# A graph network on one Trainium2 core: in the attention passes of kind "add", the sum over eight edge slots moves from TensorE and ScalarE to one strided VectorE instruction

## What is computed

```python
# layer 0, expert scorer: h is (M, HEADS=4, NUM_EXPERTS=4)
e = leaky_relu(a_src[src] + a_dst[dst], negative_slope=0.2)
ee = exp(e - segment_max(e, dst)[dst])
alpha = ee / (segment_sum(ee, dst)[dst] + 1e-16)
agg = segment_sum(h[src] * alpha[:, :, None], dst)
...
# layer 3: s is (N, 8), Vh is (N, 8, 32)
alpha = leaky_relu(s[src] + s[dst], NEG_SLOPE)
e = exp(alpha - segment_max(alpha, dst)[dst])
a = e / segment_sum(e, dst)[dst]
attn = segment_sum(Vh[src] * a[:, :, None], dst).reshape(N, D_MODEL)
```

## Time and profile before

| | us |
|---|---|
| unprofiled executions (3), median | 13737.19 |
| lowest, highest | 13736.53, 13757.31 |
| profiled execution, its own time | 13846.6 |
| profiled execution, its span | 13844.9 |
| pass `be` in it (first gather to last `add`) | about 4823 to 5915 |
| pass `ge` in it (first gather to last `add`) | about 11336 to 12861 |

### The profile page before, as it was taken

The page is one execution under the profiler, slowest core; times in us unless marked ns, Lnnn a source line. Parts: engine busy times, 40 slices in busy tenths (PEclk is TensorE's granted clock), DMA queues, the critical chain, the costliest instruction groups (busy, mean ns, idle before and its releaser), DMA issues. The chain is left out here.

```text
span 13844.9 us, 108219 instructions
## 1 busy us (share of the span) xinstructions
PE 7534.6 (54%) x30838; PEld 6003.5 (43%) x30838; DVE 6330.2 (46%) x16971; ACT 1340.8 (10%) x3400; POOL 6032.2 (44%) x6195
## 2 busy tenths in 40 slices
PE   3333433346665455586777564545544936666535
PEld 2333333335554345554566433333433835555423
DVE  6555654558886422232112245656522134454454
ACT  0000000000000100011122010000011200010001
POOL 1666366046664066603666406656301036666000
PEclk9999999777777655587788786777776967777767
DMA  1111111046666011202333602212523323336000
GB/s 41 53 51 54 38 54 44 13 139 172 178 178 134 13 8 8 8 14 68 92 90 90 60 13 48 47 41 44 27 26 97 109 58 93 95 94 86 19 7 16
DMA packets 454853, 872.00 MB, mean 63 GB/s; under 512 B 172059, under 2 KB 267149, under 8 KB 453907
## 3 DMA queue, kind: packets, MB, share of 16 engines
q0 software_dynamic: 277568, 621.62, 21.4%
q1 hardware_dynamic: 176714, 243.62, 6.1%
HBM read 820.84 MB, written 52.88 MB: 63 GB/s over the span
## 5 line engine op out<-in xcount | busy, mean ns | idle before, releaser
L552 POOL DMA_INDIRECT ee_rows<-e_table,net_mr_data x1000 | 993.6, 994 | 1038.7 <-POOLq L1656 469.2
L552 POOL DMA_INDIRECT ge_rows<-g_table,net_mr_data x1000 | 959.0, 959 | 674.2 <-issue 241.7
L855 POOL DMA_INDIRECT ce_rows<-c_table,net_mr_data x1000 | 947.2, 947 | 511.6 <-issue 245.5
L387 POOL DMA_INDIRECT main_slots<-em_load,em_where x784 | 809.6, 1033 | 642.5 <-DVE em_where L362 395.6
L552 POOL DMA_INDIRECT ae_rows<-a_table,net_mr_data x752 | 722.5, 961 | 592.5 <-POOLq L1656 202.4
L589 PE MATMUL ee_part_ps<-ee_message,net_eye 125*125 125x256 f32 x2000 | 607.8, 471 | 523.6 <-issue 300.8
L552 POOL DMA_INDIRECT be_rows<-b_table,b_br_data x728 | 696.2, 956 | 434.7 <-issue 172.9
L589 PE MATMUL ge_part_ps<-ge_rows,net_eye 125*125 125x256 f32 x2000 | 624.8, 481 | 304.7 <-ACT ge_part L650 210.2
L346 PE MATMUL em_look_ps<-em_table,em_hot_tT 25*128 25x125 f32 x1568 | 366.9, 421 | 739.3 <-issue 655.3
L589 PEld LDWEIGHTS ee_part_ps<-ee_message,net_eye 125*125 125x125 f32 x2000 | 472.7, 241 | 639.0 <-issue 542.4
L387 POOL DMA_INDIRECT gat_slots<-eg_load,eg_where x512 | 531.7, 1039 | 381.5 <-DVE eg_where L362 217.1
(11 more groups left out here) (1004 smaller groups left out, 16859.0 us busy)
## 6 DMA issues: line engine op xcount, KB each, us to landing
em_key_row<-main_keys SPq DMA_DIRECT2D x98, 512.0 KB
f_w<-in_L_ffn_W_dram SPq DMA_DIRECT2D x40, 1024.0 KB, 5.1
eg_key_row<-gat_keys SPq DMA_DIRECT2D x64, 512.0 KB
ce_rows<-c_table,net_mr_data POOLq DMA_INDIRECT x1000
ee_rows<-e_table,net_mr_data POOLq DMA_INDIRECT x1000
ge_rows<-g_table,net_mr_data POOLq DMA_INDIRECT x1000
main_slots<-em_load,em_where POOLq DMA_INDIRECT x784
ae_rows<-a_table,net_mr_data POOLq DMA_INDIRECT x752
```

Source lines behind the costliest of these rows:

```text
L387: pool.indirect_dma_start(edge["slots"], bass.IndirectOffsetOnAxis(ap=where[:, c:c + 1], axis=0), load[:, c, :], None).then_inc(scattered, 16)
L552: pool.indirect_dma_start(rows[n][:, s, :], None, table, bass.IndirectOffsetOnAxis(ap=data[:, g, s, 0:1].bitcast(I32), axis=0)).then_inc(g ...
L855: pool.indirect_dma_start(rows[:, g % RING, s, :], None, table, bass.IndirectOffsetOnAxis(ap=data[:, g, s, 0:1].bitcast(I32), axis=0)).the ...
```

## The change

In calls of kind "add" the eight identity matmuls of `sum_slots` and ScalarE's `keep` are gone. In their place DVE, in `send`, sums the eight weighted slots itself: one `reduce_sum` over the slot axis, which reads with the slots innermost (a stride of one table row, 264 or 20 floats) and writes straight into `part`. A `drain` stands ahead of it. POOL waits for `message_ready` of the group five before, as it did in kind "mix", and no longer for single slots; `scale` waits for no copy.

```diff
@@ gpsimd
                         if g >= RING:
-                            if kind == "mix":
+                            if kind != "dot":
                                 pool.wait_ge(message_ready, g - RING + 1)
                             else:
                                 pool.wait_ge(slot_summed, (g - RING) * SLOTS + s + 1)
@@ tensor
-                    if 0 <= i - 1 < G:
+                    if kind != "add" and 0 <= i - 1 < G:
                         sum_slots(i - 1)
@@ vector, send(g)
                     if g >= PARTS:
                         dve.wait_ge(totalled, g - PARTS + 1)
+                    if kind == "add":
+                        dve.drain()
+                        dve.reduce_sum(part[0:NP, g % PARTS, 0:W].rearrange("p (h v) -> p h v", h=H)[:, :, 0:dv], values(g).rearrange("p s (h v) -> p h v s", h=H), axis=AX.X)
                     dve.reduce_sum(part[0:NP, g % PARTS, 0:W].rearrange("p (h v) -> p h v", h=H)[:, :, dv], w.rearrange("p s h -> p h s"), axis=AX.X).then_inc(message_ready, 1)
@@ vector, scale(g)
-                    dve.wait_ge(part_kept, g + 1)
+                    if kind != "add":
+                        dve.wait_ge(part_kept, g + 1)
```

## The result

The changed kernel took 13,969.91 us (median of four runs, 13,958.4 to 13,974.19) against 13,745.99 for the kernel before, run four times with it: a ratio of 1.0161 [1.0144, 1.0179], 224 us slower. The prediction was 13,420, faster. It was wrong in sign.

The account below looks back on a forecast made before the run. The prediction took TensorE's slot sums to bound passes be and ge, with POOL's gathers next. From 13737.2 us, be gaining 150.3 and ge 167.9 (together 318) gave 13419, stated as 13,420; whole range 13,375 to 13,550.

Parts of the forecast that it names:

- The step that failed: TensorE in ge and be: records stretched 1.6 and 1.8 times, leaving 4.0 and 5.3 us a group, covered by POOL.
- rival C: TensorE's lateness in be and ge comes with each loop turn, not the slot sums; nothing gained, 13,737 us; chance 0.07.
- DVE's sum: DVE's new reduction takes 3.77 us a group in ge, 0.38 in be, hidden; DVE's ge group 10.3 us.
- The release: In be and ge all eight slots come free at once; POOL waits at slot 0 or not at all.
- POOL's pace: In be and ge POOL's gathers bound next, 10.1 us a group; be's 728 gathers take 918 us instead of 1056.4.
- Rival D: Gathers in ge hit their DMA limit sooner, set by pace; twenty groups more cost 80 us, 13,499; chance 0.09.
- The clock: TensorE's clock at 1.2 GHz in be and ge; ge's records at most 3.7 us a group, covered unless late.

Follow-up runs that it names:

- chip 0: Follow-up occasion on which the unaltered changed kernel ran again beside the kernel before: 12,666.89 us, ratio 1.0005 [0.9995, 1.0015].
- pe_dummy_2: Changed kernel with eight matmuls of constants per group added on TensorE in be and ge, chip 11: 14,095.71 us, 1.0253 to the kernel before.
- late_back: Changed kernel with `fall_behind` and `factors` moved one loop turn later, chip 7: 14,030.94 us, 1.0160 to the kernel before.
- cheap_sum: Changed kernel with a copy of the first slot in place of the eight-slot sum, chip 7: 13,928.21 us, 1.0083 to the kernel before.
- ge_only: Kernel before with the change made in pass ge alone, be left as before, chip 12: 12,672.26 us, 1.0006 to the kernel before.

## Why the prediction was wrong

**The step that failed** is "TensorE can't have taken more than its 12 us a group: ... By these factors 4.0 and 5.3 us are left, under cover of POOL's 10.1". It took the lateness of TensorE's results as a stretching of its work, so that fewer matmuls would mean less of it. The runs show otherwise: it is there on some occasions and not on others; where it is there, results are held while POOL gathers (162 of 599 prompt) and come when POOL pauses (102 of 112); and it doesn't go with the matmuls. What is left of TensorE's work was 2.5 us a group, as said, but most of its results did not come under cover of POOL's gathers: POOL stopped for them once a block. In `be` that makes 11.9 us a group where 10.1 was forecast, and in `ge` 13.4. This is rival C's first half, held at 0.07 and priced at 13,737. C's no change is right for `be` (1104 us against 1097). On chip 0 it is right by luck, since nothing is late there.

**DVE's sum** was right to 0.04 us, and DVE's group of 10.3 was 10.1. That it would be hidden was wrong on the late chip: DVE's 10.1 us four times, and 13 us or so of late stretch, make the 53.9 us between L757 at 12023.51 and the next at 12077.38. On chip 0 the same work is hidden, 10.53 us a group.

**The release** got no price ("POOL waits at slot 0 or not at all"). POOL waits at slot 0 for 370.3 us in `ge`, mostly 12.8 us at a time, where it had waited 144.4 in 113 steps of about one. Between the pauses it gathers for 40 us. That this lumping makes the results later than single releases did is not shown, since the release alone never ran on a late chip. What the runs suggest is this: matmuls in TensorE's order cost 126 us (pe_dummy_2's +350 less the change's +224), so taking them away should have gained about that; DVE's sum costs 103 (late_back less cheap_sum). With the gain of 126 and the cost of 103, a change that comes to +224 leaves some 247 us for the rest of it, which is the release, the copy that is gone and the signals that moved. That is arithmetic over three chips, with dummy matmuls in place of the old ones, and not a measurement. Why `ge` lost as much as it did stays open by this part.

**POOL's pace** as the next bound was right: 728 gathers of `be` take 5324.9 + 0.9 - 4412.4 = 913 us on chip 0, where 918 was said. But with `be` as before the change (ge_only, chip 12) they take 914, so nothing was there to gain; the 138 us between 918 and 1056 were never TensorE's work. **Rival D** is settled by the tail of `ge`, on the first chip and on chip 0:

```profile
12800.00:12850.00 50.00, 17.11 (x56) 12.91 (x55) 36.88 (x49) 3.22 (x14) 36.41 (x38) 0.53 1.01 82
```

```profile
11450.00:11500.00 50.00, 17.87 (x55) 13.68 (x54) 37.98 (x53) 3.65 (x15) 37.92 (x40) 0.50 1.00 82
```

The DMA share jumps when about 890 of the 1000 gathers have been issued, in the trace before (12630), in the one after (12750) and on chip 0 (11450), although POOL came there at 11.6, 13.3 and 10.2 us a group. So it belongs to what the last groups fetch and not to pace: the forecast had this right, and D not. **The clock** was at 1.2 GHz in both passes, as said, and cost nothing visible: on chip 0 it is as low (0.51) and nothing is late.

What was there to read beforehand: by the earlier trace rows the copy starts 7.5 us after the modelled end of the records in `ge` (256 columns) and 12.3 us in `be` (16 columns). The prediction calls both 10 us. Lateness that is larger behind less work speaks against stretching, and I wrote it under C without giving it weight. That the trace of one chip needn't hold for another could not be read from it.

## What to carry to other kernels

When results come long after the records that made them, don't divide the lateness by the work and expect it to shrink with the work; compare two places with different work first, ask what another engine does meanwhile, and let the rival that takes it as a constant weigh as much. Run both kernels on more than one chip before explaining a loss of a per cent or two. And where an engine issues gathers at the pace of the pass, price what each change does to that engine: when its slots come free, and what the others' operands do to its instructions.

## What the runs showed of the hardware that I had not expected

- Two kinds of times for the same kernel, 8.6 to 9.2% apart (13,746 to 13,816 us, and 12,657 to 12,662), by chip or by occasion. Only the stretches with indirect gathers differ. Between the changed kernel on the first chip and on chip 0, `ce`, which the change leaves alone, takes 1474 against 1309 us from its first to its last instruction and `ee` 1584 against 1365, while `f` takes 879 against 878 and `h` 410 against 410.
- On a late chip TensorE's signals are held, rather than its work: in the kernel before, eight semaphore events of slot sums come 0.04 us apart from 12033.04 to 12033.34, though each sum takes 0.43 us of records or more. In the changed kernel they can come in steps of 5.6 us (12012.25, 12017.84, 12023.49). On chips 0 and 12 every event of `ge` comes 0.01 to 0.02 us after its record's end. It is no matter of bandwidth: `be`, at 8 GB/s, has it as well.
- On late chips a part of TensorE's semaphore events is missing from the trace (93 of 125 are there for `turn` in `ge` after; all of them on chip 0). The waits there carry names such as "remote" or a DMA of another pass.
- What holds the signals was not found. They come at once when POOL has paused, but by which path POOL's stream of gathers has to do with it is not shown.
